# One graph kernel, four layers: the last two slot steps peeled off the loop, the ahead gather dropped, the slots extracted whole, and the first gather issued ahead of two clearings

## The chip, the cores and the metric

The kernel runs on one core of a Trainium2 chip. The metric is the time of one execution on the device, in microseconds (us). TensorE (PE, with its weight loads as PEld), VectorE (DVE), ScalarE (ACT), GpSimd (POOL) and SyncE (SP, which issues the DMAs) run their own instruction streams and wait for each other by semaphores.

## The reference

There are 64 graphs of 256 nodes with 128 features, and a sparse adjacency (about 3% of the entries, and the diagonal). Four layers run in a row, each as x + layer(relu(layernorm(x)), adj).

```python
# layer 0: degrees d = sum |adj|; elu(d^-.5 * (adj @ (x W * d^-.5)) + b)
# layer 1: hyperbolic attention: logmap, expmap, sigmoid gates on adj
# layer 2 (message passing, the part the change is about):
m_j = x @ W1[:D];  m_i = x @ W1[D:]
pre = m_j[:, None, :, :] + m_i[:, :, None, :] + b1
msg = gelu(layernorm(pre, g1, be1))                 # exact gelu
agg = einsum('bijo,bij->bio', msg, adjacency)
out = layernorm(concat([x, agg]) @ W2 + b2, g2, be2)
# layer 3: four dense graph layers with l2-normed adjacency, tanh
```

In layer 2 a message exists for each pair of nodes, and only pairs with an edge count. The kernel therefore lists each node's neighbours, and computes messages slot by slot: slot s holds the s-th neighbour of every node.

## The kernel before, in words

The 64 graphs are worked off in 16 groups of 4. One group is 8 "units" of 128 nodes. The parts of the four layers are interleaved: `mix(g)` does layer 0 of group g+2, layer 1 of g+1, the update that ends layer 2 of g, and layer 3 of g-1. After it come the steps of layer 2 of group g+1 (`slots`). Each engine has its own code for both. On DVE, ACT and POOL the groups 1 to 13 are passes of one loop (DVE: L1457), and the others are written out. PE's loop begins one group later.

**Slots.** `take_slots` (DVE, L1063) finds each node's neighbours in descending order of the edge, eight at a time: MAX8 (L1074), their indices (L1077), a copy of the values, MATCH_REPLACE8 (L1082) which strikes them out, and a cast of the indices (L1083). It is called for units 0 to 3, then for units 4 to 7. Between the two stands `ratios` (L1274), which needs POOL's totals (L626). Inside the second, after its first round, stands `clip` (L1279), which needs ACT's L890 and is needed by ACT's L904. How many slots the group needs, rounded up to whole pairs, is found in `keep_slots` (L1056) and read as a register by every engine. The number of rounds is (2 pairs + 10) // 8.

**Steps.** For every slot there is a step. SP spreads the index row over the partitions (L431); DVE turns it into a one-hot (`pick`, L1118, two instructions); ACT seeds a PSUM bank with the node's own term (`seed`, L730); PE adds the neighbour's term by multiplying with the one-hot (`gather`, L1513, 32 matmuls); DVE takes the statistics (L1136); POOL forms the variance (L578) and its power (L581); DVE normalises (L1128); POOL shifts (L570); ACT applies the gelu (L776) and makes diagonal matrices of edge weights (L781); PE aggregates into bank_d (`aggregate`, L1522). Two banks, bank_b and bank_c, alternate. Each step's gather and pick are for one or two steps ahead. So the last passes of the inner loop make one gather, two picks and a pair of seeds that nothing uses, and at the end DVE waits for that last gather. PE clears bank_b and bank_c in `start_slots` (L1841) and bank_d at the head of `slots` (L1503).

## Time and profile before

| | |
|---|---|
| median of 3 runs | 4009.07 us (4004.93 to 4012.15) |
| profiled execution, own time | 4007.12 us |
| its span | 4005.3 us |
| busy PE / DVE / ACT / POOL | 81% / 82% / 66% / 48% |
| the chain that ended last | issue 27%, PE 20%, POOL 19%, DVE 19%, ACT 9% |

The busy shares mix two kinds of stretches that take turns 16 times: the steps of a group (some 90 us), and the mixed part between (some 140 us). In the slices POOL falls to 1 or 2 tenths in one kind and rises to 7 or 8 in the other. Within the chain the largest line is POOL's shift L570, with 13% of the span.

### The profile page before, as it was taken

How to read it: one execution, taken by the hardware profiler on the slowest of the kernel's cores; microseconds unless marked ns; L12 is line 12 of the kernel's file. 1: busy time of each engine (PE TensorE's matmuls, PEld its weight loads, DVE VectorE, ACT ScalarE, POOL GpSimd, SP SyncE). 2: the span in 40 equal slices, each digit the busy share in tenths (PEclk: the TensorE clock that was granted, in tenths of full speed). 3: DMA queues.
4: the chain of work that ended last, by engine and by line, in shares of the span. 5: the costliest groups of instructions: out<-in, count | busy, mean ns of one | idle time of the engine just before them, and what ended most of it. 6: DMA issues, size and time to landing. Idle time of an engine off the chain costs nothing.

```text
span 4005.3 us, 92223 instructions
## 1 busy us (share of the span) xinstructions
PE 3231.7 (81%) x24743; PEld 2745.1 (69%) x24840; DVE 3267.3 (82%) x11961; ACT 2663.1 (66%) x6659; POOL 1939.6 (48%) x1598
## 2 busy tenths in 40 slices
PE   3484688787888889788788888888897887888888
PEld 2273667677676777767677776767777676776777
DVE  4788888888888888888888888888888888887830
ACT  2484776848667585766848676685857668495753
POOL 1182753719355382744718273461827447182730
PEclk7596889999899999989999998999999899999999
DMA  2010102012020210202011020202102020110200
GB/s 82 29 53 29 50 9 75 24 36 73 5 79 16 67 37 30 72 3 80 24 51 48 30 68 2 83 22 62 37 30 72 4 80 24 41 46 9 61 8 21
DMA packets 147064, 167.74 MB, mean 42 GB/s; under 512 B 13232, under 2 KB 100912, under 8 KB 146736
## 3 DMA queue, kind: packets, MB, share of 16 engines
q1 hardware_dynamic: 146736, 163.96, 13.5%
q8 instruction: 134, 2.20, 0.2%
q14 instruction: 194, 1.59, 0.1%
HBM read 151.33 MB, written 12.58 MB: 41 GB/s over the span
## 4 chain that ended last, share of the span: by engine, by line
issue 27%; PE 20%; POOL 19%; DVE 19%; ACT 9%; DVEq 3%; POOLq 1%; ACTq 0%; DMA 0%; SPq 0%
POOL v_z L570 13%; PE n_bank_c L1604 4%; PE n_bank_d L1621 3%; PE n_bank_d L1622 3%; POOL v_prstd L581 2%; PE n_bank_d L1618 2%; DVE v_top_at L1077 2%; POOL v_pvar L578 2%; PE n_bank_b L1679 2%; ACT v_rows L813 1%; DVE v_top L1074 1%; DVE v_normed L1168 1%; ACT v_pair L878 1%; DVE v_adj_x L1082 1%; PE n_bank_b L1835 1%
## 5 line engine op out<-in xcount | busy, mean ns | idle before, releaser
L570 POOL TENSOR_TENSOR v_z<-v_z,all_bc_L_gnn_be 128x512 f32<-128x512 f32 x620 | 787.1, 1271 | 50.5 <-DVE v_z L1128 24.2
L781 ACT ACTIVATE v_diag<-all_ident,v_value 128x128 f32<-128x128 f32 x2480 | 754.0, 386 | 0.0
L1522 PE MATMUL n_bank_d<-v_diag,v_msg 128*128 128x128 f32 x4960 | 637.8, 283 | 31.0 <-ACT v_diag L781 29.9
L1522 PEld LDWEIGHTS n_bank_d<-v_diag,v_msg 128*128 128x128 f32 x4960 | 594.3, 196 | 36.7 <-ACT v_diag L781 32.9
L581 POOL TENSOR_TENSOR v_prstd<-v_pvar,all_neg_half 128x8 f32<-128x8 f32 x310 | 578.9, 1868 | 25.8
L1513 PE MATMUL n_bank_b<-v_parts,v_onehot 128*128 128x128 f16 x5472 | 379.9, 227 | 181.1 <-ACT n_bank_b L730 180.9
L1513 PEld LDWEIGHTS n_bank_b<-v_parts,v_onehot 128*128 128x128 f16 x5472 | 327.4, 101 | 236.1 <-ACT n_bank_b L730 231.2
L1604 PE MATMUL n_bank_c<-all_l_wsd,v_fT 128*128 128x256 f32 x1792 | 449.6, 393 | 29.3 <-ACT v_adjT L715 26.8
L1513 PE MATMUL n_bank_c<-v_parts,v_onehot 128*128 128x128 f16 x4960 | 339.2, 224 | 131.8 <-ACT n_bank_c L730 131.1
L725 ACT ACTIVATE v_fT<-n_bank_d,all_l_c 128x256 f32<-128x256 f32 x256 | 119.9, 474 | 462.3 <-PE n_bank_d L1622 462.1
L1128 DVE SCALAR_TENSOR_TENSOR v_z<-n_bank_c,v_prstd,all_bc_L_gnn_g 128x128 f32<-128x128 f32 x1240 | 345.3, 342 | 89.5 <-POOL v_prstd L581 89.4
L1128 DVE SCALAR_TENSOR_TENSOR v_z<-n_bank_b,v_prstd,all_bc_L_gnn_g 128x128 f32<-128x128 f32 x1240 | 346.4, 341 | 85.1 <-POOL v_prstd L581 84.5
L1513 PEld LDWEIGHTS n_bank_c<-v_parts,v_onehot 128*128 128x128 f16 x4960 | 289.2, 100 | 181.6 <-ACT n_bank_c L730 181.6
L1604 PEld LDWEIGHTS n_bank_c<-all_l_wsd,v_fT 128*128 128x128 f32 x1792 | 355.4, 198 | 67.6
L776 ACT ACTIVATE v_msg<-v_z 128x512 f32<-128x512 f32 x620 | 381.3, 615 | 7.9 <-POOL v_z L570 7.9
L635 POOL TENSOR_TENSOR v_s_norm<-v_s_norm2c,v_half 128x8 f32<-128x8 f32 x16 | 28.0, 1750 | 706.8 <-DVE v_s_norm2c L1327 706.8
L1621 PE MATMUL n_bank_d<-v_adjT,v_sd 128*128 128x256 f32 x1024 | 325.8, 402 | 0.0
L1622 PE MATMUL n_bank_d<-v_adj_l,v_sd 128*128 128x256 f32 x1024 | 322.8, 399 | 0.0
L721 ACT ACTIVATE v_sd<-n_bank_c 128x512 f32<-128x512 f32 x256 | 150.8, 594 | 256.4 <-PE n_bank_c L1604 255.1
L730 ACT ACTIVATE n_bank_b<-v_own 128x512 f32<-128x512 f32 x342 | 202.4, 592 | 173.2 <-DVE v_z L1128 169.6
L1118 DVE TENSOR_SCALAR v_onehot<-v_spread,v_node_of 128x1024 f16<-128x1024 bf16 x684 | 298.4, 478 | 7.5 <-DMA v_spread<-slot_rows 7.5
L1136 DVE BATCH_NORM_STATS2 v_pstats<-n_bank_b 128x6 f32<-128x256 f32 x620 | 232.4, 418 | 41.6 <-PE n_bank_b L1513 32.7
(277 smaller groups left out, 6617.3 us busy)
## 6 DMA issues: line engine op xcount, KB each, us to landing
v_spread<-slot_rows SPq DMA_DIRECT2D x342, 256.0 KB, 3.2
v_adj_l<-in_adj SPq DMA_DIRECT2D x128, 256.0 KB, 4.0
v_adj_x<-in_adj SPq DMA_DIRECT2D x64, 256.0 KB, 3.7
v_ring<-in_x SPq DMA_DIRECT2D x16, 512.0 KB, 5.6
out_x<-v_xout SPq DMA_DIRECT2D x64, 128.0 KB, 1.9
slot_rows<-v_indexT SPq DMA_DIRECT2D x16, 256.0 KB, 2.0
w_wu<-in_L_gnn_wu SPq DMA_DIRECT2D x4, 192.0 KB, 2.5
all_W<-in_L_gnn_W SPq DMA_DIRECT2D x2, 128.0 KB, 4.0
```

The source lines that it names most:

```text
L570: nc.gpsimd.tensor_tensor(z[par][:, units], z[par][:, units], wide(bc["L2_gnn_be1"])[:, units], ALU.add).then_inc(sem["z_ready"], 1)
L581: nc.gpsimd.tensor_tensor(prstd[:, par], pvar[:], minus_half, ALU.pow).then_inc(sem["prstd_ready"], 1)
L776: nc.scalar.activation(msg[par][:, units], z[par][:, units], ACT.Gelu).then_inc(sem["msg_ready"], 1)
L781: ins = nc.scalar.activation(diag[par][:, u], ident[:], ACT.Copy, scale=value[:, u, bass.ds(slot, 1)])
L1118: ins = v.tensor_scalar(onehot[:, par, k], spread[:, par], node_of[:, k:k + 1], None, ALU.is_equal)
L1128: ins = v.scalar_tensor_tensor(z[par][:, u], ps_m[par][:, u], prstd[:, par, u:u + 1], bc["L2_gnn_g1"][:], ALU.mult, ALU.mult)
L1136: ins = v.bn_stats(pstats[:, par, two].rearrange("p u c -> p (u c)"), ps_m[par][:, 2 * two:2 * two + 2].rearrange("p u d -> p d u"))
L1513: ins = nc.tensor.matmul(ps_m[par][:, u], onehot[:, par, k, u * P:(u + 1) * P], parts[:, b * NB + k, t], start=False, stop=False, skip_gro ...
L1522: ins = nc.tensor.matmul(ps_agg[:, u // NB, (u % NB) * P:(u % NB + 1) * P], msg[par][:, u], diag[par][:, u], start=False, stop=False, skip ...
L1604: ins = nc.tensor.matmul(ps_l3[b % 2][:, k], fT[:, b, L3_SLOT[f], k * P:(k + 1) * P], keep["l3_wsd"][:, sum(L3_IN[:l]) + i, :], start=Fals ...
L1621: nc.tensor.matmul(acc, sd[:, b, k, 0:D], rowT[:, b, k], start=False, stop=False)
L1622: ins = nc.tensor.matmul(acc, sd[:, b, k, D:2 * D], colA[:, b, k], start=False, stop=k == NB - 1)
```

## The change: what it does

1. The stored count is now two lower (and at least 7), and the last two steps stand behind the inner loop on DVE, ACT and PE. There the gather, picks and seeds of the step ahead are left out, and so are their index spreads. The counts of semaphores lose their terms in the group's number. The number of steps is the same. On ACT the last diagonals stand ahead of the last two gelus.
2. `take_slots` handles all 8 units in each round. `ratios` stands behind round 0, and `clip` behind all rounds and behind the signal `index_ready`. The number of rounds is (2 body + 9) // 8, where body is one less than pairs, so it covers the steps exactly.
3. PE issues the first gather of a group in `start_slots`, ahead of the clearing of bank_c, the wait for x, and the clearing of bank_d.

```diff
@@ first_spreads, second_spreads and slots of SyncE; POOL and ACT alike
-                n = sp.value_load(n_slots[0:1, bass.ds(a, 1)], min_val=7, max_val=N)
-                sp.reg_mov(n_pairs, (n + 1) // 2)
+                n = sp.value_load(n_slots[0:1, bass.ds(a, 1)], min_val=7, max_val=N - 2)
+                sp.reg_mov(n_body, (n + 1) // 2)
...
-                before = sp.snap(sp.snap(count) + a * 2)
-                with sp.Fori(2, pairs + 1) as i:
+                before = sp.snap(count)
+                with sp.Fori(2, body + 1) as i:
...
-                sp.reg_add(count, count, pairs * 2)
+                sp.reg_add(count, count, sp.snap(body * 2 + 2))
@@ slots of GpSimd
-                pairs = pool.snap((n + 1) // 2)
+                pairs = pool.snap((n + 1) // 2 + 1)
@@ slots of ScalarE
-                def act_step(par, step, slot, second=False):
-                    act.wait_ge(sem["z_made"], step * 2 + 1)
-                    seed(1 - par, 0)
+                def act_step(par, step, slot, second=False, last=False):
+                    if not last:
+                        act.wait_ge(sem["z_made"], step * 2 + 1)
+                        seed(1 - par, 0)
...
-                with act.Fori(1, pairs) as i:
+                with act.Fori(1, body) as i:
...
-                act.reg_add(count, count, pairs * 2)
+                act.reg_add(count, count, body * 2)
+                ending = act.snap(count)
+                for par in range(2):
+                    act_step(par, act.snap(ending + par), act.snap(body * 2 + par), last=par == 1)
+                act.reg_add(count, count, 2)
                 after = act.snap(count)
                 gelu(0, act.snap(after - 1), 1)
+                diagonals(1, after, act.snap(body * 2 + 1))
                 gelu(1, after, 0)
-                diagonals(1, after, act.snap(pairs * 2 - 1))
                 gelu(1, after, 1)
@@ keep_slots and take_slots of VectorE
-                v.tensor_scalar(n_slots[0:1, bass.ds(a, 1)], needed_g[:], 7.0, float(N), ALU.max, ALU.min)
+                v.tensor_scalar(needed_g[:], needed_g[:], float(N), -2.0, ALU.min, ALU.add)
+                dve.drain()
+                v.tensor_scalar(n_slots[0:1, bass.ds(a, 1)], needed_g[:], 7.0, None, ALU.max)
...
-            def take_slots(a, part_, between=None):
-                units = range(part_ * HALF, (part_ + 1) * HALF)
+            def take_slots(a, between):
...
-                full = dve.snap(((n + 1) // 2 * 2 + 10) // 8 - 1)
+                full = dve.snap(((n + 1) // 2 * 2 + 9) // 8 - 1)
...
-                    for u in units:
+                    for u in range(UNITS):
...
                 eight(0, True)
-                if between:
-                    between()
+                between()
...
@@ slots of VectorE
-                def dve_step(par, step, first=False):
+                def dve_step(par, step, first=False, last=False):
...
-                    pick(dve.snap(step + g * 2 + 2), par)
+                    if not last:
+                        pick(dve.snap(step + 2), par)
...
-                with dve.Fori(1, pairs) as i:
+                with dve.Fori(1, body) as i:
...
+                ending = dve.snap(count)
+                for par in range(2):
+                    dve_step(par, dve.snap(ending + par), last=True)
+                dve.reg_add(count, count, 2)
                 after = dve.snap(count)
-                dve.wait_ge(sem["gathered"], (after + g) * 2 + 2)
@@ mix of VectorE
-                    take_slots(a, 0)
-                    ratios()
-                    take_slots(a, 1, between=clip)
+                    take_slots(a, between=ratios)
                     dve.drain().then_inc(sem["index_ready"], 1)
+                    clip()
@@ slots of TensorE
-                for half_ in range(2):
-                    pe.wait_ge(sem["parts_ready"], g * GB + 2 * half_ + 2)
-                    gather(0, pe.snap(before + g), half_)
...
+                def pe_step(par, step, first=False, second=False, last=False):
+                    if not last:
+                        pe.wait_ge(sem["onehot_ready"], step + 2)
+                        gather(1 - par, pe.snap(step + 1), 0)
+                        gather(1 - par, pe.snap(step + 1), 1)
...
+                with pe.Fori(1, body) as i:
...
+                for par in range(2):
+                    pe_step(par, pe.snap(ending + par), last=par == 1)
@@ start_slots of TensorE
                     for i in range(2):
                         pe.wait_ge(sem["own_ready"], a * GB + 2 * i + 2)
+                        if i == 1:
+                            pe.wait_ge(sem["onehot_ready"], after + 1)
+                            for half_ in range(2):
+                                pe.wait_ge(sem["parts_ready"], a * GB + 2 * half_ + 2)
+                                gather(0, after, half_)
                         for c in range(2):
                             ins = nc.tensor.matmul(ps_m[i][:, c * HALF:(c + 1) * HALF], zero16[:, 0:P], zero16[:],
                                                    start=True, stop=False, skip_group_check=True)
```

PE at a group's start in the loop, before: from the clearing of bank_b to the first gather (v_fT is layer 3's output being turned, v_zero_410 the zeros that clear a bank).

```order
L1841 MATMUL n_bank_b<-v_zero_410 128x512 x2
L1814 ISA
L1816 MATMUL n_bank_d<-all_ident,v_fT 128x128 x2
L1814 REGISTER_ALU
L1816 MATMUL n_bank_d<-all_ident,v_fT 128x128 x2
L1839 REGISTER_ALU
L1841 MATMUL n_bank_c<-v_zero_410 128x512 x2
L1854 REGISTER_ALU
L1503 MATMUL n_bank_d<-v_zero_410 128x512 x2
L1504 ISA
L1508 ISA
L1513 MATMUL n_bank_b<-v_parts,v_onehot 128x128 x16
```

The same place after.

```order
L1851 MATMUL n_bank_b<-v_zero_410 128x512 x2
L1820 ISA
L1822 MATMUL n_bank_d<-all_ident,v_fT 128x128 x2
L1820 REGISTER_ALU
L1822 MATMUL n_bank_d<-all_ident,v_fT 128x128 x2
L1844 REGISTER_ALU
L1846 REGISTER_ALU
L1510 ISA
L1515 MATMUL n_bank_b<-v_parts,v_onehot 128x128 x16
L1510 REGISTER_ALU
L1515 MATMUL n_bank_b<-v_parts,v_onehot 128x128 x16
L1851 MATMUL n_bank_c<-v_zero_410 128x512 x2
```

The first gather (32 matmuls, two rows) has moved ahead of the clearing of bank_c and, behind these rows, of bank_d; the second gather stays behind both.

DVE in the extraction, before: the end of the first half's call, `ratios`, and the head of the second's.

```order
L1074 MAX v_top<-v_adj_x 128x8 x4
L1077 MAX_INDEX v_top_at<-v_top,v_adj_x 128x8 x4
L1078 ISA x2
L1078 COPY v_value<-v_top 128x4x8
L1083 ISA
L1083 COPY v_index<-v_top_at 128x4x8
L1274 TENSOR_TENSOR v_pair<-v_pair 128x512 x4
L1069 TENSOR_LOAD v_n_slots
L1069 ISA x2
L1074 MAX v_top<-v_adj_x 128x8 x4
L1077 MAX_INDEX v_top_at<-v_top,v_adj_x 128x8 x4
L1078 COPY v_value<-v_top 128x4x8
```

The same place after.

```order
L1080 MAX v_top<-v_adj_x 128x8 x8
L1083 MAX_INDEX v_top_at<-v_top,v_adj_x 128x8 x8
L1084 COPY v_value<-v_top 128x8x8
L1088 MATCH_REPLACE v_adj_x<-v_top,v_adj_x 128x256 x8
L1089 CAST v_index<-v_top_at 128x8x8
L1283 TENSOR_TENSOR v_pair<-v_pair 128x512 x4
L1095 UNCONDITIONAL_BRANCH
L1080 MAX v_top<-v_adj_x 128x8 x8
L1083 MAX_INDEX v_top_at<-v_top,v_adj_x 128x8 x8
L1084 ISA
L1084 COPY v_value<-v_top 128x8x8
```

Each round now has eight of each instruction, and `ratios` follows the first round of all units instead of the last round of half of them.

DVE at the end of a group's steps, before: the last rows of the loop, its branch, and what follows.

```order
L1136 BN_STATS v_pstats<-n_bank_c 128x6 x2
L1144 REGISTER_ALU
L1128 SCALAR_TENSOR_TENSOR v_z_424<-n_bank_b,v_prstd,all_bc_L_gnn_g 128x128 x4
L1116 ISA
L1118 TENSOR_SCALAR v_onehot<-v_spread,v_node_of 128x1024 x2
L1150 ISA
L1150 COMPARE_AND_BRANCH
L1153 ISA
L1155 REGISTER_ALU
L1157 REGISTER_ALU
L1158 ISA
L1128 SCALAR_TENSOR_TENSOR v_z_425<-n_bank_c,v_prstd,all_bc_L_gnn_g 128x128 x4
```

The same place after: the last peeled step.

```order
L1139 ISA
L1141 BN_STATS v_pstats<-n_bank_c 128x6 x2
L1145 REGISTER_ALU
L1133 SCALAR_TENSOR_TENSOR v_z_424<-n_bank_b,v_prstd,all_bc_L_gnn_g 128x128 x4
L1139 REGISTER_ALU
L1141 BN_STATS v_pstats<-n_bank_c 128x6 x2
L1133 SCALAR_TENSOR_TENSOR v_z_424<-n_bank_b,v_prstd,all_bc_L_gnn_g 128x128 x4
L1163 ISA
L1167 ISA
L1133 SCALAR_TENSOR_TENSOR v_z_425<-n_bank_c,v_prstd,all_bc_L_gnn_g 128x128 x4
```

No pick (L1118 before) stands behind the last statistics any more, and the branch stands two steps earlier.

## Rows read from the trace of the kernel before

**Rows 1.** Page, part 5, costliest groups: busy, mean ns of one, idle before
```profile
L581 POOL TENSOR_TENSOR v_prstd<-v_pvar,all_neg_half 128x8 f32<-128x8 f32 x310 | 578.9, 1868 | 25.8
...
L1513 PE MATMUL n_bank_b<-v_parts,v_onehot 128*128 128x128 f16 x5472 | 379.9, 227 | 181.1 <-ACT n_bank_b L730 180.9
...
L1118 DVE TENSOR_SCALAR v_onehot<-v_spread,v_node_of 128x1024 f16<-128x1024 bf16 x684 | 298.4, 478 | 7.5 <-DMA v_spread<-slot_rows 7.5
```

**Rows 2.** Timeline, one steady step of a group: start us, us, what [idle before]
```profile
2151.62 0.87 DVE L1118 TENSOR_SCALAR v_onehot<-v_spread,v_node_of 128x1024 f16<-128x1024 bf16 x2
2151.73 1.87 POOL L581 TENSOR_TENSOR v_prstd<-v_pvar,all_neg_half 128x8 f32<-128x8 f32 x1
...
2156.58 1.88 POOL L581 TENSOR_TENSOR v_prstd<-v_pvar,all_neg_half 128x8 f32<-128x8 f32 x1
```

**Rows 3.** Timeline, a first step whose pick came late
```profile
1620.58 1.64 POOL L581 TENSOR_TENSOR v_prstd<-v_pvar,all_neg_half 128x8 f32<-128x8 f32 x1
1620.60 0.88 DVE L1118 TENSOR_SCALAR v_onehot<-v_spread,v_node_of 128x1024 f16<-128x1024 bf16 x2 [0.50 <-DMA v_spread<-slot_rows]
```

**Rows 4.** Windows between two aggregates, DVE at L1074: us, busy (count), clock
```profile
762.93:1019.62 256.69, 11.23 (x32) 0.93 0.14 43
1963.87:2193.25 229.38, 8.41 (x24) 0.93 0.14 43
```

**Rows 5.** The same windows, POOL at L581
```profile
762.93:1019.62 256.69, 41.07 (x22) 0.93 0.14 43
1963.87:2193.25 229.38, 33.71 (x18) 0.93 0.14 43
```

**Rows 6.** Timeline of DVE, extraction of the first group
```profile
128.23 1.41 DVE L1074 MAX8 v_top<-v_adj_x 128x8 f32<-128x256 f32 x4 [0.63 <-issue]
...
139.09 1.41 DVE L1074 MAX8 v_top<-v_adj_x 128x8 f32<-128x256 f32 x4 [0.50 <-issue]
...
142.82 2.50 DVE L1274 TENSOR_TENSOR v_pair<-v_pair 128x512 f32<-128x512 f32 x4
...
161.05 1.12 DVE L1021 SCALAR_TENSOR_TENSOR v_hn<-n_bank_a,v_norm,all_bc_L_gnn_b 128x128 f32<-128x128 f32 x4 [0.18 <-issue]
```

**Rows 7.** Timelines of DVE, POOL and ACT, extraction in a loop pass
```profile
2007.36 1.41 DVE L1074 MAX8 v_top<-v_adj_x 128x8 f32<-128x256 f32 x4 [0.42 <-issue]
...
2023.01 3.39 DVE L1274 TENSOR_TENSOR v_pair<-v_pair 128x512 f32<-128x512 f32 x4
...
2044.77 2.16 DVE L1021 SCALAR_TENSOR_TENSOR v_hn<-n_bank_a,v_norm,all_bc_L_gnn_b 128x128 f32<-128x128 f32 x8 [0.27 <-issue]
...
2019.10 4.95 POOL L626 TENSOR_TENSOR v_total<-v_pair 128x512 f32<-128x512 f32 x4 [16.57 <-ACT v_pair L878]
...
2044.03 0.63 ACT L904 ACTIVATE v_pair<-v_pair 128x512 f32<-128x512 f32 x1
```

**Rows 8.** Timeline of ACT, the same part in the unrolled pass
```profile
3655.14 3.90 ACT L878 ACTIVATE v_pair<-v_pair 128x1024 f32<-128x1024 f32 x4
...
3678.49 0.63 ACT L904 ACTIVATE v_pair<-v_pair 128x512 f32<-128x512 f32 x1
```

**Rows 9.** Chain and timelines, start of a group in the loop
```profile
2094.09 1.47 issue
2095.56 0.06 DVEq L1457
...
2096.44 1.42 DVE L1136 BATCH_NORM_STATS2 v_pstats<-n_bank_b 128x6 f32<-128x256 f32 x4 [2.36 <-PE n_bank_b L1513]
2098.24 0.88 DVE L1118 TENSOR_SCALAR v_onehot<-v_spread,v_node_of 128x1024 f16<-128x1024 bf16 x2 [0.37 <-DMA v_spread<-slot_rows]
...
2093.79 1.95 PE L1513 MATMUL n_bank_b<-v_parts,v_onehot 128*128 128x128 f16 x32
```

**Rows 10.** Timeline of DVE, start of the first group
```profile
210.22 1.65 DVE L1136 BATCH_NORM_STATS2 v_pstats<-n_bank_b 128x6 f32<-128x256 f32 x4 [1.24 <-PE n_bank_b L1513]
```

**Rows 11.** Timeline of PE, end of a group's steps
```profile
1953.02 4.09 PE L1522 MATMUL n_bank_d<-v_diag,v_msg 128*128 128x128 f32 x32
```

More of the change, by code:

```diff
@@ L1499, in layer0_out, with gather @@
                 ins.then_inc(sem["out_made"], 1)
+            def gather(par, number, half_):
+                pe.wait_ge(sem["seeded"], number * 2 + (half_ + 1))
+                for u in range(half_ * HALF, (half_ + 1) * HALF):
+                    b = u // NB
+                    for k in range(NB):
+                        for t in range(2):
+                            ins = nc.tensor.matmul(ps_m[par][:, u], onehot[:, par, k, u * P:(u + 1) * P],
+                                                   parts[:, b * NB + k, t], start=False, stop=False,
+                                                   skip_group_check=True)
+                ins.then_inc(sem["gathered"], 1)
             def slots(g):
@@ L1524, in aggregate @@
                     ins.then_inc(sem["summed"], 1)
[L1526 to L1536 removed]
+                def pe_step(par, step, first=False, second=False, last=False):
+                    if not last:
+                        pe.wait_ge(sem["onehot_ready"], step + 2)
+                        gather(1 - par, pe.snap(step + 1), 0)
+                        gather(1 - par, pe.snap(step + 1), 1)
                     if not (first or second):
```

91 lines of the change are left out of this document (36 added, 55 removed).

## The prediction

> **What bounds the kernel now.** I read the page's costliest groups first, then the timeline of a steady step, then windows between aggregates, then the extraction, then the two borders of a group's steps. The groups give the counts [rows 1]: POOL's power ran 310 times, so there are 310 steps in 16 groups. The one-hots number 684 = 2 x 342, which is 32 picks more than steps, two per group. The gathers of bank_b number 5472 / 32 = 171, against 310 / 2 = 155 steps on that bank: 16 more, one per group. These surpluses are what part 1 of the change drops.
>
> A steady step is POOL's [rows 2]: two powers start 4.85 us apart, and between them POOL does the power (1.87) and the shifts. DVE, ACT and PE wait inside each step. So a gather, a seed or a pick that is dropped is worth nothing by its own duration: 16 gathers of 1.95 us, 31 us of PE, are hidden.
>
> The mixed part between steps is bound by a chain that changes engine. In a pass of the loop DVE's extraction lies from 2007.36 to 2044.77, and ACT's artanh L904 starts at 2044.03 [rows 7]; DVE is the later by little there, and what delays it delays the pass.
>
> **Part by part. (a) Two picks dropped.** In a steady step the pick starts 0.11 us ahead of the power, which then takes 1.87. Where the pick started behind it, the power took 1.64 [rows 2, 3]. The mean over 310 is 1868 ns [rows 1], so nearly all steps pay. The power is on the path in the last two steps too: statistics, variance, power, normalise, shift, gelu, aggregate. Without the picks these two are 0.23 us shorter each: 16 x 0.46 = 7.4 us. Bounds: 0 (the 1.64 had another cause) and, were the whole pick of 0.87 in the way, 16 x 2 x 0.3 = 10.
>
> The Trainium skill ("SBUF — State Buffer", Who interferes with whom) has DVE and GpSimd share a port pair under an exclusive lock, held for the whole instruction, with the later one fully blocked. The first of the rows agrees (the power grows by 0.23, less than one pick instruction's 0.48); the second does not, since a pick that starts 0.02 behind the power still takes 0.88. By the rule the power would gain about one pick instruction less its lead, 0.37 a time and 12 us in all; by the rows it is the 7.4 above.
>
> **(b) Extraction in the 13 loop passes.** A half round costs 5.43 on average, (139.09 - 128.23) / 2, and the last one, without the strike, 142.82 - 139.09 = 3.73 [rows 6]. The whole-unit rounds have the same instructions but half the drains, copies and casts, some 0.9 us each: 2 x 5.3 - 0.9 = 9.7 for the first, 2 x 5.55 - 0.95 = 10.2 for the middle, 2 x 3.73 - 0.75 = 6.7 for the last. The first ends at 2007.36 + 9.7 = 2017.1, where `ratios` now stands. It needs POOL's totals, which begin at 2019.10 and end at 2024.05 [rows 7]. So DVE waits 2 us at least, and runs in step with POOL. `ratios` took 3.39 us beside the totals and 2.50 alone [rows 6, 7]. I take its end at 2026.4, as now. Then come 0.2 + 10.2 + 6.7, ending at 2043.6, and `clip`, 1.4 us, to 2045.0, against 2044.77: 0.2 us later, 13 x 0.2 = -2.6 us. If `ratios` ends right behind the totals (2024.8), the pass gains up to 1.4, of which ACT's artanh, at 2044.03 in any case, leaves 0.3 to 0.5. If it ends a further 1 us later, the loss is 1.2 a pass. The first `clip` instruction ends near 2044.0, so the artanh is just not delayed.
>
> **(c) The fourth round of group 3.** With 22 steps [rows 5] the old rule gives (22 + 10) // 8 = 4 rounds and the new (22 + 7) // 8 = 3 (body is 10, and 2 body + 9 = 29). The rows show 32 MAX8 in that window and 24 in the other [rows 4]. The windows differ by 27.3 us, of which four steps are 4 x 4.85 = 19.4. The rest is the round: +7.9 us. Groups of 18 and 20 steps have 3 rounds by either rule.
>
> **(d) Extraction ahead of the first two groups.** Here nothing holds DVE: 32.8 us from 128.23 to 161.05 [rows 6], of which ratios 2.4 and clip 1.35 stay; 29.05 becomes 0.2 + 9.7 + 10.2 + 6.7 = 26.8. Twice 2.2: +4.4 us (2 to 5).
>
> **(e) The first gather ahead.** In the first group the gather is the late one: statistics at 210.22 waited 1.24 us for PE [rows 10]. It could move ahead by two clearings, some 0.9 us, and in the second group 0.5: +1.4. In the 12 groups whose steps follow the loop's back edge the same wait reads 2.36 us [rows 9], and the row of waits puts it down to PE. But PE's gather began at 2093.79 and ended at 2095.74, 0.7 us before the statistics at 2096.44. The chain shows DVE's own issue from 2094.09 and the loop's branch L1457 at 2095.56. DVE is late by its own back edge, so the gather ahead gives nothing: 0 (upper end under the rivals). The second gather moves back by two clearings less one gather's lead, some 0.2 us, and has over 1 us to spare.
>
> **(f) The unrolled pass ahead of group 15.** ACT has no layer 0 there: artanh comes 3678.49 - 3655.14 = 23.35 us after its logarithms began [rows 8], while by (b) the first clip is done some 26 after them. ACT is held about 2.7, of which slack in PE's turns takes some: -1.4 (from -2.7 to +0.3).
>
> **(g) ACT's last diagonals earlier.** In most groups what comes next is DVE's chain and not the aggregate; in the last one the update waits for it: +0.7. **(h)** One more tensor_scalar and drain per group: -0.3 where it is on the path.
>
> Sum: 7.4 - 2.6 + 7.9 + 4.4 + 1.4 - 1.4 + 0.7 - 0.3 = 17.5 us. The profiled execution took 4007.1, so 3989.6 for it; it stood 2 below the median 4009.1, which gives 3991.6. I write 3991. Steps, PE's work for layers 0, 1 and 3, and their clock stay as they are.
>
> **The rivals.** *A: the gather ahead frees DVE in the loop too.* For it: the wait's own label. Against it: the ends above. Even then the third pick, which waits for its index at 2098.24 [rows 9], with statistics behind it, caps the gain at 0.57 a group (normalise cannot begin before 2099.8): 12 x 0.56 = 6.7, so 3985.
>
> *B: `ratios` and totals do not disturb each other when interleaved one by one.* Then (b) turns to +0.3 a pass and (f) to 0: 2.6 + 3.9 + 1.4, so about 3984. For it: the instructions could alternate. Against it: 3.39 against 2.50 now.
>
> *C: the last powers are not shorter*, because in those steps the power was stretched by something else (the normalise that follows, the other reads of DVE): (a) is 0, giving 3998 to 3999.
>
> *D: slower. The inner loop is left two steps early.* The next two steps are straight code behind it that must be fetched. The price, if it is that of the outer back edge: DVE's pause of 2.36 us [rows 9], less 0.5 us of slack, for each of 16 exits on each engine in turn; with DVE alone 16 x 1.9 = 30, less the 17.5: 4021. It decides from 17.5 / 16 = 1.1 us an exit. Against it: today's exits show no such gap; PE's last aggregates run through as 32 matmuls in 4.09 us across the loop's end [rows 11].
>
> The Trainium skill ("Runtime: NRT & Kernel Launch", Instruction fetch mechanics) says that a taken branch to a target outside the window of two pages forces a fetch, and that sequential code is prefetched. The back edge's 1.47 us of issue agrees. By that rule leaving the loop costs nothing, while a larger outer body changes nothing either.
>
> *E: `ratios` ends 1 us later in every pass.* DVE catches POOL's every total, and the rounds behind it slide: 13 us lost, leaving 4.5 gained: 4004 to 4005, no change.
>
> **Chances.** Forecast 0.56, A 0.07, B 0.15, C 0.12, E 0.05, D 0.05. A difference under 0.2%, 8 us, cannot be told from none, so "same" is 4001 to 4017. Forecast, A, B and C lie below 4001, but C and the forecast with its lower bounds reach it: faster 0.86, same 0.08, slower 0.06. The forecast's own range is 3983 to 3998: (a) 0 to 10, (b) -15 to +5. With the others it is 3978 to 4002.
>
> **What will show it.** POOL's mean at L581 falls slightly, and its last two powers of each group read near 1.64. One-hots are 620, gathers of bank_b 4960, MAX8 384. The window at group 3 shrinks by some 8 more than its neighbours. `ratios` in a loop pass begins after a wait for POOL near 2.6 us into the totals, and the next layer-0 line (L1021 before) starts within 0.5 us of its former distance from the first MAX8, 37.4. The wait of the first statistics in loop passes stays at 2.4 and keeps its wrong name. The forecast fails if any exit of the inner loop shows a gap over 1 us, if ACT waits for clip before its artanh in loop passes, or if that 37.4 becomes 38.5.

## The result, and the profile after

The changed kernel takes 3952.66 us (median of 4 runs, 3950.47 to 3955.3), the kernel before in the same session 4010.61 (4004.93 to 4014.43): a ratio of 0.9857 [0.984, 0.9874]. The spans are 3953.5 and 4005.3. The forecast was 3991, so the gain is 58 us where 17.5 were expected, and the time lies below the range.

The page's costliest groups show that the work itself changed as forecast: 310 powers as before, and 620 one-hots where there were 684; the gathers of bank_b number 4960 (line engine op, then busy us, mean ns | idle before) [rows 1].

```profile
L581 POOL TENSOR_TENSOR v_prstd<-v_pvar,all_neg_half 128x8 f32<-128x8 f32 x310 | 576.7, 1860 | 25.8
...
L1123 DVE TENSOR_SCALAR v_onehot<-v_spread,v_node_of 128x1024 f16<-128x1024 bf16 x620 | 271.6, 482 | 23.6 <-DMA v_spread<-slot_rows 23.6
```

**The steady step is shorter.** The timeline of DVE and POOL in the step that answers to [rows 2] (start us, duration):

```profile
2118.41 1.13 DVE L1133 SCALAR_TENSOR_TENSOR v_z<-n_bank_c,v_prstd,all_bc_L_gnn_g 128x128 f32<-128x128 f32 x4 [0.47 <-POOL v_prstd L581]
...
2116.50 1.88 POOL L581 TENSOR_TENSOR v_prstd<-v_pvar,all_neg_half 128x8 f32<-128x8 f32 x1
...
2121.24 1.88 POOL L581 TENSOR_TENSOR v_prstd<-v_pvar,all_neg_half 128x8 f32<-128x8 f32 x1
...
2140.27 1.65 POOL L581 TENSOR_TENSOR v_prstd<-v_pvar,all_neg_half 128x8 f32<-128x8 f32 x1
```

Two powers are 4.74 us apart, not 4.85. The power is no shorter; the normalise starts 2118.41 - 2118.38 = 0.03 us behind its end. In the step of [rows 2] it came 0.13 behind: the power ends at 2153.60, and DVE's row there, waiting 0.57 instead of 0.47, is

```profile
2153.73 0.61 DVE L1128 SCALAR_TENSOR_TENSOR v_z<-n_bank_c,v_prstd,all_bc_L_gnn_g 128x128 f32<-128x128 f32 x2 [0.57 <-POOL v_prstd L581]
```

The last two powers of the group, without a pick beside them, take 1.65 (at 2140.27 and 2144.79).

**TensorE's clock stays up at the turns.** Late in every loop pass PE turns `normed` (L1825 before, L1830 now) and multiplies it with the weights (L1835, L1840). Before, DVE's node statistics and then PE read as follows.

```profile
2064.64 1.13 DVE L1318 SCALAR_TENSOR_TENSOR v_tangent<-n_bank_b,v_s_kb,v_hn 128x128 f32<-128x128 f32 x4
...
2078.59 1.65 DVE L985 BATCH_NORM_STATS2 v_nstats<-v_ring 128x6 f32 x8 [0.49 <-issue]
...
2084.24 0.66 PE L1825 MATMUL n_bank_b<-all_ident,v_normed 128*128 128x128 f32 x4 [1.71 <-DVE v_normed L1103]
2085.26 1.12 PE L1825 MATMUL n_bank_b<-all_ident,v_normed 128*128 128x128 f32 x4 [0.37 <-DVE v_normed L1103]
...
2087.03 2.67 PE L1835 MATMUL n_bank_b<-all_W,v_hT 128*128 128x256 f32 x8
```

After, the same rows:

```profile
2032.48 1.13 DVE L1327 SCALAR_TENSOR_TENSOR v_tangent<-n_bank_b,v_s_kb,v_hn 128x128 f32<-128x128 f32 x4
...
2046.17 1.65 DVE L991 BATCH_NORM_STATS2 v_nstats<-v_ring 128x6 f32 x8
...
2051.83 0.66 PE L1830 MATMUL n_bank_b<-all_ident,v_normed 128*128 128x128 f32 x4 [1.22 <-DVE v_normed L1108]
2052.85 0.66 PE L1830 MATMUL n_bank_b<-all_ident,v_normed 128*128 128x128 f32 x4 [0.37 <-DVE v_normed L1108]
...
2053.78 1.89 PE L1840 MATMUL n_bank_b<-all_W,v_hT 128*128 128x256 f32 x8
```

DVE's 0.49 us "issue" ahead of the statistics is down to 0.14, and PE is idle 1.22 us ahead of the turns instead of 1.71. Only about half of that difference is the stall's. Counted from the tangents (the first row of each view), the turns begin 0.25 earlier (19.35 us behind them instead of 19.60), and PE's own work of layer 3 ends 0.24 later (18.13 instead of 17.89). The second turn takes 0.66 instead of 1.12. The windows over these rows give the granted clock (us, PE busy (count), clock, DMA share, GB/s), first before, then after:

```profile
2084.00:2088.00 4.00, 3.39 (x15) 0.65 0.00 0
```

```profile
2052.00:2056.00 4.00, 3.63 (x23) 1.00 0.11 31
```

Before, the clock falls to the lower of its two levels (1.2 GHz, of 2.4) in the middle of the turns; now it does not. From the first turn's start to the start of the last parts (DVE L1110, now L1115) it is 7.6 to 7.7 us before in 12 of 13 loop passes, and 6.0 in all of them after.

**The first steps of a group are longer.** DVE's waits (us in total, times, longest), before and after:

```profile
DVE v_onehot L1118 <- DMA v_spread<-slot_rows: 7.5, 11, 1.8
```

```profile
DVE v_pstats L1141 <- issue: 27.8, 12, 2.5
DVE v_onehot L1123 <- DMA v_spread<-slot_rows: 23.6, 14, 3.8
...
DVE v_needed L1058 <- issue: 5.7, 13, 0.4
```

The index row of the third step lands late in nearly every group. And the wait which [rows 9] put down to PE now reads "issue" at about the same length, as DVE's timeline shows:

```profile
2062.28 1.42 DVE L1141 BATCH_NORM_STATS2 v_pstats<-n_bank_b 128x6 f32<-128x256 f32 x4 [2.22 <-issue]
```

**The account.** The program's last power starts at 3822.35 before and at 3768.43 after, 53.9 us earlier. Between the two traces that comes from:

| stretch | us |
|---|---|
| regular steps of groups 1 to 15, 4.85 to 4.75 each | -23.1 |
| last gap of each of them, 4.85 to 4.53 | -4.9 |
| first two gaps of each of them | +11.8 |
| turns to last parts, 12 loop passes | -19.3 |
| fourth round of group 3 | -8.0 |
| pass ahead of group 1, and all ahead of the first power | -5.6 |
| pass ahead of group 15, up to its last parts | +2.6 |
| first statistics of the unrolled groups 14 and 15 | -1.6 |
| the rest, by difference | -5.8 |

Behind the last power 2.1 us are lost. Two rows hold 42 us that the prediction did not have.

### The profile page after: what moved, and what is told of

Same layout as the page of the kernel before. It is cut to its first block, busy times and chain, and to the rows that moved or that the text cites. A ratio compares the mean times of both kernels' runs of the same rounds, so it can differ in the third digit from the quotient of the medians.

```text
span 3953.5 us, 90024 instructions
## 1 busy us (share of the span) xinstructions
PE 3191.1 (81%) x24327; PEld 2701.1 (68%) x24328; DVE 3230.3 (82%) x11773; ACT 2644.7 (67%) x6627; POOL 1949.1 (49%) x1598
## 4 chain that ended last, share of the span: by engine, by line
issue 27%; PE 25%; POOL 20%; DVE 14%; ACT 10%; DVEq 2%; POOLq 1%; ACTq 0%; DMA 0%; SPq 0%
POOL v_z L570 14%; PE n_bank_c L1610 6%; PE n_bank_d L1627 4%; PE n_bank_d L1628 3%; PE n_bank_d L1624 3%; POOL v_prstd L581 2%; POOL v_pvar L578 2%; ACT v_rows L819 2%; PE n_bank_b L1685 2%; PE n_bank_c L1606 1%; PE n_bank_a L1499 1%; DVE v_normed L1177 1%; ACT v_pair L884 1%; ACT v_junk L683 1%; DVE v_top_at L1083 1%
## 5 line engine op out<-in xcount | busy, mean ns | idle before, releaser
L1530 PE MATMUL n_bank_d<-v_diag,v_msg 128*128 128x128 f32 x4960 | 627.5, 280 | 54.9 <-ACT v_msg L776 27.6
L1530 PEld LDWEIGHTS n_bank_d<-v_diag,v_msg 128*128 128x128 f32 x4960 | 583.9, 193 | 63.0 <-issue 32.4
L581 POOL TENSOR_TENSOR v_prstd<-v_pvar,all_neg_half 128x8 f32<-128x8 f32 x310 | 576.7, 1860 | 25.8
L1515 PE MATMUL n_bank_b<-v_parts,v_onehot 128*128 128x128 f16 x4960 | 346.8, 228 | 164.3 <-ACT n_bank_b L730 152.4
L1515 PEld LDWEIGHTS n_bank_b<-v_parts,v_onehot 128*128 128x128 f16 x4960 | 299.3, 102 | 213.0 <-ACT n_bank_b L730 211.4
L1123 DVE TENSOR_SCALAR v_onehot<-v_spread,v_node_of 128x1024 f16<-128x1024 bf16 x620 | 271.6, 482 | 23.6 <-DMA v_spread<-slot_rows 23.6
L730 ACT ACTIVATE n_bank_b<-v_own 128x512 f32<-128x512 f32 x310 | 183.7, 593 | 128.6 <-DVE v_z L1133 125.0
L1624 PE MATMUL n_bank_d<-v_fT,all_l_wn 128*128 128x256 f32 x896 | 254.3, 402 | 18.1 <-ACT v_fT L725 16.5
```

The costliest lines, as they stand in the source:

```text
L581: nc.gpsimd.tensor_tensor(prstd[:, par], pvar[:], minus_half, ALU.pow).then_inc(sem["prstd_ready"], 1)
L1123: ins = v.tensor_scalar(onehot[:, par, k], spread[:, par], node_of[:, k:k + 1], None, ALU.is_equal)
L1515: ins = nc.tensor.matmul(ps_m[par][:, u], onehot[:, par, k, u * P:(u + 1) * P], parts[:, b * NB + k, t], start=False, stop=False, skip_gro ...
L1530: ins = nc.tensor.matmul(ps_agg[:, u // NB, (u % NB) * P:(u % NB + 1) * P], msg[par][:, u], diag[par][:, u], start=False, stop=False, skip ...
L1624: nc.tensor.matmul(acc, keep["l3_wn"][:, sum(L3_IN[:l]) + i, :], fT[:, b, L3_SLOT[f]], start=i == 0, stop=False)
```

## The experiments

Two theories for the steps. **R:** DVE's stream had one more instruction between POOL's power and the normalise. In `slots` the count for the semaphore `gathered`, (step + g)·2 + k, and the one for `msg_ready`, step·2 + 1, were two register values. Now both are step·2 + 1, one value made once. So the rows between statistics and normalise lost `L1141 ISA`:

```
before: L1136 BN_STATS v_pstats   L1140 REGISTER_ALU   L1141 ISA   L1128 SCALAR_TENSOR_TENSOR v_z
after:  L1141 BN_STATS v_pstats   L1145 REGISTER_ALU               L1133 SCALAR_TENSOR_TENSOR v_z
```

The trace before shows what L1141 is (DVE's sequencer, count, duration in ns min/median/max, first and last start in us):

```profile
L1141 DVEq FUSED_REGOPS  x277: 46/46/71, 429.5 to 3819.4; - x139
L1141 DVEq EVENT_SEMAPHORE  x17: 21/21/21, 212.1 to 288.8; - x17
```

In the 277 steps of groups 1 to 15 it is a register instruction, and the trace names it, and not the normalise, as what waits for the power. In the step of [rows 2] it starts at 2153.64, 0.04 us behind the power's end, takes 0.05, and the normalise, with the wait for `msg_ready`, comes 0.04 later. In the 17 steps of the first group the wait for `msg_ready` is an instruction of its own that runs ahead, while the power is still under way, and the normalise waits for the power itself. After, all steps are of that kind:

```profile
L1146 DVEq EVENT_SEMAPHORE  x294: 21/21/21, 211.2 to 3764.4; - x147
```

From the power's end to the normalise the median is 0.13 us before in groups 1 to 15, and 0.03 to 0.04 in its first group and in all groups after.

**The rival:** the peeled steps, the dropped picks or the shorter loop body made each step shorter. For the turns: **S**, DVE's stall sets PE's idle time and so the clock, against an earlier or later cause on PE's own side.

**1. The offset given back.** After, but `gathered` starts 14 higher, and DVE's count for it is 14 higher too; nothing else moves.

```diff
-                        dve.wait_ge(sem["gathered"], step * 2 + (half_ + 1))
+                        dve.wait_ge(sem["gathered"], (step + 7) * 2 + (half_ + 1))
...
+            pe.sem_inc(sem["gathered"], 14)
```

> The changed kernel, with the gathers' semaphore started 14 higher and VectorE waiting for (step + 7) * 2 + k. No work is added, only the two counts that VectorE waits for are no longer the same expression, so a register instruction stands again between the wait for the power and the normalise. Theory R (the 0.10 us a steady step come from that register instruction): the step is 4.85 us again in every group, the first one included, some 276 x 0.10 = 27 us slower than the changed kernel, near 3980. Rival (the step got shorter because of the dropped gathers and picks, or because of SyncE's and TensorE's simpler counts): the step stays at 4.75 and the time near 3953.

Measured 4005.66, ratio 0.9992 [0.9983, 1.0002]. POOL's timeline, in group 8:

```profile
2130.74 1.88 POOL L581 TENSOR_TENSOR v_prstd<-v_pvar,all_neg_half 128x8 f32<-128x8 f32 x1
...
2135.59 1.88 POOL L581 TENSOR_TENSOR v_prstd<-v_pvar,all_neg_half 128x8 f32<-128x8 f32 x1
```

The step is 4.85 again, with everything peeled, and in the first group too, and the register instruction stands in all 294 steps (L1146). R holds. But the whole gain of 53 us went, some 26 more than was expected of the steps: DVE's stall is back as well (0.43 us at L994, 13 times, in its waits), PE is idle 1.72 ahead of the turns, and they are slow in 13 of 13 passes.

**2. The two waits swapped, in the kernel before.** The wait for the power comes last, directly ahead of the normalise.

```diff
-                            dve.wait_ge(sem["prstd_ready"], step + 1)
                             dve.wait_ge(sem["msg_ready"], step * 2 + 1)
+                            dve.wait_ge(sem["prstd_ready"], step + 1)
```

> The kernel before, with VectorE's two waits ahead of the first normalise in the other order: msg_ready first, prstd_ready last. Theory R: the last instruction that waits for the power is then the normalise itself, so the step falls from 4.85 to 4.75 in the groups 1 to 15, and the time by 26 us, to near 3984. The first group, at 4.75 before, stays. Rival (the simpler counts of all engines together, or the peeled end): no change, 4010.

Measured 3982.08, 0.9939 [0.9922, 0.9955]: 28 us from two lines in another order, though the four runs lie 17.5 us apart (3974.76 to 3992.29). POOL's timeline:

```profile
2117.54 1.88 POOL L581 TENSOR_TENSOR v_prstd<-v_pvar,all_neg_half 128x8 f32<-128x8 f32 x1
...
2122.30 1.88 POOL L581 TENSOR_TENSOR v_prstd<-v_pvar,all_neg_half 128x8 f32<-128x8 f32 x1
```

4.76 with the old loop, the old picks and the same power. The rival is out. In this trace the steps give 24 us and the mixed parts 7: DVE's stall at the node statistics is gone here too (0.14 instead of 0.49), though no work was taken away. PE is still idle 1.32 us ahead of the turns, and they are slow in 10 of 13 passes.

**3. A delay ahead of the node statistics.** After, with one DVE instruction of 0.43 us there, to put back what the stall took.

```diff
+                    v.tensor_scalar(pair[:, 0, 0], pair[:, 0, 0], 1.0, None, ALU.mult)
                     node_stats(a)
```

> The changed kernel, with one VectorE instruction of 0.43 us added ahead of the node statistics (L991), which nothing uses. Theory C (the kernel before lost TensorE's clock because TensorE stood idle 1.7 us instead of 1.2 there, which put the turns and the node terms at the lower clock): the idle time grows to about 1.65, the clock falls again behind it in most of the 13 loop passes, and the time grows by 13 x (0.4 + 1.6) = 26 us, to 3979. Rival (the clock has another reason, such as the work of the pass before): 14 to 15 x 0.4 = 6 us, 3959, with the node terms at full clock.

Measured 3994.2, 0.9957 [0.9941, 0.9974]: 41.5 us more than after, from 13 x 0.43 = 5.6 us of work, and beyond what was expected. PE's timeline:

```profile
2069.54 0.66 PE L1831 MATMUL n_bank_b<-all_ident,v_normed 128*128 128x128 f32 x4 [1.91 <-DVE v_normed L1108]
```

The idle time is 1.91 and not 1.7: a stall of 0.43 has come up at L1102 too, so both delay `normed`. All 13 turns are slow. They account for some 21 us, and their start 0.7 later in each pass for 9; the other 11 were not traced. The edit moved the code as well, and so does not price the delay by itself.

**4. PE kept busy.** The kernel before, with four matmuls on zeros into bank_c in PE's idle time; nobody reads them.

```diff
+                    if l3:
+                        pe.wait_ge(sem["sd_kept"], (t + 1) * (4 * GB))
+                        for c in range(4):
+                            nc.tensor.matmul(ps_m[1][:, (c % 2) * HALF:(c % 2 + 1) * HALF], zero16[:, 0:P], zero16[:],
+                                             start=True, stop=True, skip_group_check=True)
```

> The kernel before, with four matmuls of zeros into bank_c put into TensorE's idle time ahead of the turns of the normed features. Theory C: the idle time ahead of the turns falls from 1.7 to below 1 us, the turns and node terms run at full clock in all passes, parts come 1.6 us earlier in 12 passes: 4010 - 19 = 3991. Rival (the clock falls whatever TensorE does in that gap): no change, 4010, or some us slower.

Measured 4002.93, 0.9981 [0.9972, 0.9991], 7 us of the 19. PE's timeline:

```profile
2079.17 0.66 PE L1830 MATMUL n_bank_b<-all_ident,v_normed 128*128 128x128 f32 x4 [0.85 <-DVE v_normed L1103]
2080.20 0.66 PE L1830 MATMUL n_bank_b<-all_ident,v_normed 128*128 128x128 f32 x4 [0.37 <-DVE v_normed L1103]
```

With DVE's stall left in place the turns run at full clock in 13 of 13 passes: it is the idle time, and the stall only through it. But the first MAX8 of 10 passes now comes 57 us behind the last power instead of 55.8. Ahead of it the clock is low in two stretches, in both kernels. They are of the same length, but lie 2 us later with the filler (ahead of group 6 they start 22.9 and 43.4 us behind the last power, instead of 21.0 and 41.4). Whether that is what gives back most of the gain, and why they come later, was not found.

**5. Part 2 alone** (the extraction), in the kernel before; the old rule for the rounds.

```diff
...
-                    take_slots(a, 0)
-                    ratios()
-                    take_slots(a, 1, between=clip)
+                    take_slots(a, between=ratios)
                     dve.drain().then_inc(sem["index_ready"], 1)
+                    clip()
```

> The kernel before with the second part of the change alone: the extraction over all eight units in each round, ratios behind round 0, clip behind all. The rule for the number of rounds stays as before, so group 3 keeps its fourth round. My step (d) as recorded gives 4.4 us for the first two groups, (b) -2.6 for the loop passes. The changed trace shows 3.6 us ahead of group 1 and 0.4 in a loop pass. If the changed code also moves VectorE's stall of 0.49 us at the node statistics, TensorE keeps its clock and 12 x 1.6 come on top. So 4010 - 10 = 4000 with the stall in place, 3975 to 3982 without it.

Measured 3990.02, 0.9955 [0.9938, 0.9972], 19 us. The step stays 4.85; the stall at the node statistics is gone, PE's idle time is 1.21 (1.44 in one pass) and no turn is slow. The part that the prediction put at +0.4 us in all brings the 19.3 of the clock. It shortens DVE's stream ahead of the statistics; that this is how it moves the stall is argued only.

**6. Part 3 alone** (the gather ahead), in the kernel before.

```diff
@@ slots of TensorE
-                pe.wait_ge(sem["onehot_ready"], first_ahead + 1)
-                for half_ in range(2):
-                    pe.wait_ge(sem["parts_ready"], g * GB + 2 * half_ + 2)
-                    gather(0, pe.snap(before + g), half_)
...
@@ start_slots of TensorE
                         pe.wait_ge(sem["own_ready"], a * GB + 2 * i + 2)
+                        if i == 1:
+                            pe.wait_ge(sem["onehot_ready"], first_ahead + 1)
+                            for half_ in range(2):
+                                pe.wait_ge(sem["parts_ready"], a * GB + 2 * half_ + 2)
+                                gather(0, pe.snap(after + a), half_)
```

> The kernel before with the third part of the change alone: the first gather of a group ahead of the clearings. By my step (e): 1 to 2 us gained in the first two groups, none in the loop, 4009. By the rival that takes the wait's label at its word: 12 x 0.6 more, 4002. VectorE's instructions are the same as before, so the step stays 4.85 and the clock still falls at the turns.

Measured 4014.83, 1.0019 [1.001, 1.0029]: slower by 6 us. DVE's wait for the index rows goes from 7.5 to 17.2 us, and the first gap of groups 1 to 15 from 72.9 to 75.6 in sum.

**7. After without part 3.**

```diff
+                pe.wait_ge(sem["onehot_ready"], before + 1)
+                for half_ in range(2):
+                    pe.wait_ge(sem["parts_ready"], g * GB + 2 * half_ + 2)
+                    gather(0, before, half_)
                 pe_step(0, before, first=True)
...
-                        if i == 1:
-                            pe.wait_ge(sem["onehot_ready"], after + 1)
-                            for half_ in range(2):
-                                pe.wait_ge(sem["parts_ready"], a * GB + 2 * half_ + 2)
-                                gather(0, after, half_)
```

> The changed kernel without its third part: the first gather stands at the head of the steps again. By step (e) within 2 us of the changed kernel, 3953 to 3955; by the rival 3960. The steady step stays 4.75.

Measured 3949.04, 0.9855 [0.9838, 0.9871]: 3.6 us under after by the medians, which the ratios (0.9855 and 0.9857) can't tell apart, and 6.0 us earlier at the last power of the trace. The wait reads

```profile
DVE v_onehot L1123 <- DMA v_spread<-slot_rows: 7.9, 9, 2.2
```

and the first gaps of groups 1 to 15 sum to 72.4 us, where after has 81.6. So part 3 costs about 6 us by run 6 and by the traces, and no part of the gain is its own.

**8. The pick behind the power.** After, but the pick waits until POOL has the variance, and one tiny instruction and a drain stand ahead of it.

```diff
+                        if not first:
+                            dve.wait_ge(sem["pvar_ready"], step + 1)
+                            v.tensor_scalar(needed_g[:], node_of[0:1, 0:1], 1.0, None, ALU.mult)
+                            dve.drain()
                         pick(dve.snap(step + 2), par)
```

> The changed kernel with VectorE's pick held until POOL's variance is there, and for one tiny instruction and a drain more, so that the pick starts behind the power and not 0.1 us ahead of it. If what stretches the power from 1.65 to 1.88 us is a pick that is already running when the power starts (my step (a)), the power takes 1.65 in the steady steps too, and the step falls from 4.75 to about 4.55: 260 x 0.2 = 50 us, near 3900. Rival (any pick beside the power stretches it, whichever starts first): the power stays at 1.88 and the time is 3953 or, with the delay on VectorE's path, up to 20 us more.

Measured 3929.43, 0.9798 [0.9782, 0.9814]. The timeline of DVE and POOL:

```profile
2090.34 0.88 DVE L1123 TENSOR_SCALAR v_onehot<-v_spread,v_node_of 128x1024 f16<-128x1024 bf16 x2 [0.16 <-issue]
...
2090.09 1.65 POOL L581 TENSOR_TENSOR v_prstd<-v_pvar,all_neg_half 128x8 f32<-128x8 f32 x1
...
2094.63 1.65 POOL L581 TENSOR_TENSOR v_prstd<-v_pvar,all_neg_half 128x8 f32<-128x8 f32 x1
```

The pick starts 0.25 behind the power, takes its usual 0.88, and the power takes 1.65; the step is 4.54. That settles (a): a pick at the power's start costs 0.23. In the trace the steps win 57 us, and the passes lose 36 of them: a stall of 0.42 us (L994) is back, PE is idle 1.71, 13 turns are slow. The Trainium skill ("SBUF — State Buffer", Who interferes with whom) has the later of the two engines blocked for the whole instruction of the other. The rows here do not show it: the pick, the later one, is not held at all.

**9. The third spread earlier.** After, but SyncE issues the index row of the third step ahead of the stores of layer 3.

```diff
+                if l1:
+                    second_spreads(g + 1, (0,))
                 if l3:
...
-                    second_spreads(g + 1)
+                    second_spreads(g + 1, (1,))
```

> The changed kernel with SyncE issuing the third index spread of a group ahead of the four stores of the output instead of behind them. In the changed trace VectorE's third pick waits 23.6 us in all for this transfer (7.5 before the change), and the first two powers of a group stand 5.4 us apart on average instead of 4.6. Theory S (the transfer lands late because it is issued late and among the loads behind it): the wait falls to a few us and the time by 8 to 12 us against the changed kernel, to 3942. Rival (the distance has another bound, such as TensorE's second gather): no change, 3953.

Measured 3946.7, 0.9843 [0.9827, 0.986]: 6 us under after by the medians, 11 at the last power of the trace. All 16 first gaps are 4.62 us (2059.76 to 2064.38 in group 8):

```profile
2059.76 1.75 POOL L583 TENSOR_TENSOR v_prstd<-v_pvar,all_neg_half 128x8 f32<-128x8 f32 x1
...
2064.38 1.88 POOL L583 TENSOR_TENSOR v_prstd<-v_pvar,all_neg_half 128x8 f32<-128x8 f32 x1
```

The longer first gap was the third index row, and nothing else.

**10. Empty instructions in after's stream.** Twelve increments of a semaphore that nobody waits for, on DVE, at the head of the mixed part.

```diff
                 if l1:
+                    for pad in range(12):
+                        dve.sem_inc(keep["held"], 1)
                     clamp_pair(3)
```

> The changed kernel with twelve empty semaphore instructions on VectorE ahead of clamp_pair(3), where it waits 1.4 us for TensorE anyway. Nothing is computed more and no count changes. Theory P (VectorE stalls 0.4 to 0.5 us at a fixed place of its instruction stream; in the changed kernel this falls beside the wait for POOL's nrstd, and twelve instructions more move it back to the node statistics, as in the kernel before): the stall shows at L991 or L994, TensorE idles 1.7 us ahead of the turns, the clock falls there, and each of the 13 loop passes takes some 2 us more: 3975 to 3980. Rival (the stall is not a matter of place): within 3 us of 3953.

Measured 3950.65, 0.9853 [0.9836, 0.9869]: nothing, no slow turn, and the stall at L1058, 0.4 us in each of 13 passes of after where it costs nothing, is gone too. That the stall moves by a plain count of instructions is not borne out here.

**11. Late pick, early spread and no gather ahead together** (the diffs of 7, 8 and 9).

> The changed kernel without its third part (the gather ahead), with the late pick and with the early spread: steps of 4.55 us (57 us less), first distances of 4.6 (9 us less). The late pick alone ended at 3929, since its mixed parts took 36 us more with the clock falling at the turns; if that stays, 3918 to 3922; if VectorE's stall moves off the node statistics, 3895.

Measured 3925.93, 0.9794 [0.9773, 0.9814]. The steps are worth another 5 us, the stall (0.43, L996) and the 13 slow turns stay.

**12. The same with the four matmuls of 4.**

> The same with four matmuls of zeros in TensorE's idle time ahead of the turns. By theory C the turns and the node terms keep full clock in every pass; by the run of the filler on the kernel before, where part of that came back as a later start of the extraction, 7 of 19 us stayed: 3905 to 3913, and 3895 if all of it stays. Rival: same as without the filler.

Measured 3899.3, 0.973 [0.9711, 0.9749]. PE's timeline at the turns:

```profile
2023.29 0.66 PE L1845 MATMUL n_bank_b<-all_ident,v_normed 128*128 128x128 f32 x4 [0.85 <-DVE v_normed L1110]
2024.32 0.66 PE L1845 MATMUL n_bank_b<-all_ident,v_normed 128*128 128x128 f32 x4 [0.37 <-DVE v_normed L1110]
```

No slow turn, and the mixed parts sum to 2158.7 instead of 2184.8 us; 21 of these 26 us lie between the turns and the last parts. It is 53 us below after, 109 below before, and the best of all.

**13 and 14. Empty instructions in the kernel before**: the edit of 10 with `range(12)` and with `range(48)`.

> The kernel before with twelve empty semaphore instructions on VectorE ahead of clamp_pair(3). The padding of the changed kernel did not bring the stall back (recorded expectation 3975, measured 3951), so the reverse is tried. If VectorE's 0.49 us ahead of the node statistics are a matter of where its instructions lie, it goes from L985 to another line, TensorE's idle time ahead of the turns falls from 1.7 to 1.2 us and the node terms keep the full clock: about 2 us less in 12 passes, 3985 to 3990. If it belongs to L985 itself (a wait the trace does not name), nothing changes: 4008.

> The same with 48 of them, which take some 1 to 2 us of VectorE's own time ahead of clamp_pair(3), where it waits 1.4. If place decides, the stall is again elsewhere than at 12, and the time goes with PE's idle time ahead of the turns: near 3990 where it is 1.2 us, near 4010 or a few us more where it is 1.7. If it belongs to L985: 4008 to 4025.

With 12: 4044.44, 1.0087 [1.0071, 1.0104], 35 us slower. The stall has left L985, but one of 1.8 to 2.3 us stands inside the first statistics of a group, on DVE's path:

```profile
2110.55 0.43 DVE L1136 BATCH_NORM_STATS2 v_pstats<-n_bank_b 128x6 f32<-128x256 f32 x1 [2.48 <-PE n_bank_b L1515]
2112.81 1.09 DVE L1136 BATCH_NORM_STATS2 v_pstats<-n_bank_b 128x6 f32<-128x256 f32 x3 [1.83 <-issue]
```

and PE is idle 1.59, with 12 slow turns. From the last parts to the first power of a group it is 8.0 to 8.5 us in 12 groups, instead of 6.0 to 6.4; the first MAX8 also comes 0.9 us later a pass. With 48: 3990.6, 0.9951 [0.9934, 0.9968], 19 us faster than the kernel before, for 48 instructions that do nothing. The stall is gone, and PE is idle 1.29 ahead of the turns,

```profile
2075.23 0.66 PE L1827 MATMUL n_bank_b<-all_ident,v_normed 128*128 128x128 f32 x4 [1.29 <-DVE v_normed L1103]
```

with one slow turn. So a kernel's stalls, and with them its clock, hang on where its instructions stand, without any work removed. Over all 16 traces of the study (13 loop passes each), by PE's idle time ahead of the turns: 0.4 to 0.9 us, none of 26 passes slow; 1.2 us, none of 66; 1.3 us, 11 of 24; 1.44 us, none of 1; 1.55 to 1.9 us, 88 of 91.

Are the stalls fetches of instructions? The traces record the packets of the queues that carry instructions, and they agree with it. Before, a packet of queue q14 starts 0.67 to 0.96 us behind the restart at L985 in 13 of 13 passes; after, one starts 0.47 to 0.74 us behind the restart at L1058, in 13 of 13, and none stands near the node statistics. In run 2, where the stall there is gone, the packet starts 1.1 to 1.4 us behind the statistics' start instead, inside a row of instructions that runs through. With the 12 empty instructions one starts within 0.4 us of the beginning of each of the 12 long stalls, in the rows above at 2110.77. The stretch 2110.60 to 2112.81 of run 13 has two (queue, kind: packets, MB, share of 16 engines):

```profile
q14 instruction: 2, 0.02, 3.4%
```

## Why the prediction was wrong

**The step that failed** is the sentence that the steps "stay as they are", and behind it that the simpler counts of semaphores (part 1 of the change) were costed at nothing. It held durations and dependences, and left out the instructions of the sequencer between a wait and what it releases: here a register instruction that carried the wait for the power, 0.10 us a step. These are 23 us in the regular steps of groups 1 to 15, and 1.5 more in their last gaps. It could have been read from the trace of before: in the first group, where g is 0 and both counts are one value, POOL's powers stood 4.75 apart already.

```profile
217.03 1.88 POOL L581 TENSOR_TENSOR v_prstd<-v_pvar,all_neg_half 128x8 f32<-128x8 f32 x1
...
221.78 1.88 POOL L581 TENSOR_TENSOR v_prstd<-v_pvar,all_neg_half 128x8 f32<-128x8 f32 x1
```

One steady step, of group 8, had been taken for all.

**The second failure** is that PE's work and its clock "stay as they are". The chain is: PE idle 1.7 us instead of 1.2, half of it by DVE's stall and half by where PE's own work ends, then the lower clock, 19.3 us. Run 5 shows which part of the change brings it; run 4 shows that work in PE's idle time keeps the clock up at the turns, with the stall left where it was. Run 2 shows that the stall is not the whole of it: without it PE is idle 1.32, and 10 of 13 turns are slow. That the stall is DVE fetching instructions is borne out by its moving with empty ones (runs 13, 14) and by the packets, but no run forced a fetch by itself.

**(a) right.** The last two powers are 1.65, and run 8 shows the cause. In run 1, where the step is 4.85, the last gap is 4.62: 0.23 for one of the two powers, as forecast. The other lies behind the last gap and was not priced by itself. Rival C falls.
**(b) wrong in sign, small.** `ratios` does run in step with the totals: it waits 3.48 us, starts 1.38 behind them and takes 5.62, as this row shows (the layer-0 line L1027 follows at 2012.09).

```profile
1988.49 5.62 DVE L1283 TENSOR_TENSOR v_pair<-v_pair 128x512 f32<-128x512 f32 x4 [3.48 <-POOL v_total L626]
```

But from the first MAX8 (1975.45) to L1027 it is 36.64 us, where it was 37.4, so 0.8 less and not 0.2 more. Of the 1.0 us that the forecast was off, 0.4 lie ahead of the end of `ratios` and the rest in the rounds and `clip` behind it. Little of it comes through: from the first MAX8 to the tangents it is 57.03 us instead of 57.28.
**(c) right**: 7.9 forecast; from the first MAX8 to the tangents the pass ahead of group 3 took 8.0 us more than its neighbours, and takes no more now. **(d) with the first part of (e)**: 5.8 forecast, 5.6 measured.
**(e) in the loop right, and incomplete.** The gather ahead gives nothing there, since DVE comes late by its own branch. In groups 14 and 15, which stand outside the loop and which the prediction left out, the first statistics no longer wait for PE: 0.8 us each. The label of the wait in the loop, which the prediction expected to stay wrong, turned into "issue". That the third index row would come later was not seen: it makes most of the +11.8 us of the first two gaps (runs 6, 7, 9). Rival A falls. Why the row lands later with the gather ahead stays open.
**(f) too small**: 2.6 us lost up to the last parts, not 1.4. **(g), (h)** can't be read off: the stretch behind the last power varies from 182.9 to 187.5 us among the traces. **Rival B** falls with the row above, **D** since the steps run on across the loop's exit (last gaps 4.76 and 4.52), **E** with (b).
**Left open:** at which length of DVE's stream a stall falls on which line (run 10 missed), why PE's own work ends 0.24 us later against the tangents, and why holding the clock at the turns moved its low stretches ahead of the first MAX8 (run 4).

## What to carry to other kernels

Read what stands between the last wait and the instruction on the path, register instructions too, and put the wait that ends last directly ahead of it: 0.10 us in each of 277 steps were two swapped lines. Where one iteration has another period than the rest (here the first group), find out why before forecasting that the period stays. When TensorE is idle ahead of a burst of matmuls, look at the granted clock of the burst; a few matmuls on zeros in the gap gave 27 us in one kernel (run 12 against run 11) and 7 in another (run 4).

## What the runs showed that was not expected

Twelve empty instructions on DVE made the kernel before 35 us slower, and 48 made it 19 us faster. A register instruction that carries the late wait costs 0.10 us a step, and whether it does is decided by two counts being one expression or not. A pick that starts 0.11 us ahead of POOL's power lengthens it by 0.23, one that starts 0.25 behind it by nothing, and is not held itself. The Trainium skill ("Runtime: NRT & Kernel Launch", Instruction fetch mechanics) has straight code prefetched and the cost of crossing a block mostly hidden. DVE's stalls of 0.49 and 1.83 us stand in straight code, with a packet of instructions beside each; if they are fetches, these rows are where it was not hidden.
